# Second attention: mixing products in two parts, maxima in four places

## The reference, cut to what matters

```python
B, S, H = (2, 256, 512)             # the kernel gets x as 1 x 1024 x 512
hd = H // HEADS                      # 32 heads of 16
scale = 1.0 / np.sqrt(hd)
qkv = x @ attn_qkvw + attn_qkvb
...
scores = jnp.einsum('bhqd,bhkd->bhqk', q, k) * scale
probs = jax.nn.softmax(scores, axis=-1)
ctx = jnp.einsum('bhqk,bhkd->bhqd', probs, v)
```

## Time and profile before

| | us |
|---|---|
| runs of the kernel before | 1608.85, 1609.5, 1614.17 |
| their median | 1609.5 |
| span of the profiled execution, first to last instruction | 1606.4 |
| median less span | 3.1 |

### The profile page before, as it was taken

The page is one execution under the profiler, slowest core; times in us unless marked ns, Lnnn a source line. Parts: engine busy times, 40 slices in busy tenths (PEclk is TensorE's granted clock), DMA queues, the critical chain, the costliest instruction groups (busy, mean ns, idle before and its releaser), DMA issues. The chain is left out here.

```text
span 1606.4 us, 22430 instructions
## 1 busy us (share of the span) xinstructions
PE 1492.6 (93%) x8030; PEld 981.8 (61%) x8030; DVE 1023.0 (64%) x2013; ACT 821.6 (51%) x1487; POOL 291.7 (18%) x276
## 2 busy tenths in 40 slices
PE   6866999999999999977979999899899999999998
PEld 4645777766677776656868888787453333333355
DVE  5744666666666666643553343364687998999646
ACT  5325666666666666632221212223316777777854
POOL 2762111111211111100000000001410243342221
PEclk9987999999999999998989999999998999999999
DMA  4142222121212221124312111105730444430001
GB/s 138 53 193 73 76 75 69 64 69 64 69 63 80 90 70 40 34 86 156 105 63 75 59 60 40 53 1 152 189 67 5 68 81 79 80 67 15 19 11 53
DMA packets 63154, 116.57 MB, mean 73 GB/s; under 512 B 12814, under 2 KB 32398, under 8 KB 61758
## 3 DMA queue, kind: packets, MB, share of 16 engines
q1 hardware_dynamic: 62692, 114.23, 24.4%
q10 hardware_dynamic: 288, 0.79, 0.3%
q0 software_dynamic: 64, 0.11, 0.0%
HBM read 82.78 MB, written 29.66 MB: 70 GB/s over the span
## 5 line engine op out<-in xcount | busy, mean ns | idle before, releaser
L1882 DVE TENSOR_REDUCE ah_minus_half<-ah_ring 128x1 f32<-128x512 f32 x512 | 321.8, 680 | 58.5 <-PE ah_ring L1788 57.1
L968 DVE CUSTOM_DVE_ANT_0 mh_score<-mh_score,mh_mask 128x128 f32<-128x128 f32 (+7 forms) x256 | 195.9, 765 | 179.1 <-PE mh_score L781 179.0
L1852 ACT ACTIVATE ah_probs<-ah_score 128x1024 f32<-128x1024 f32 x256 | 248.7, 1024 | 69.5 <-PE ah_score L1805 68.8
L890 ACT ACTIVATE mh_probs<-mh_score,mh_minus_max 128x128 f32<-128x128 f32 (+7 forms) x256 | 189.8, 741 | 39.7 <-DVE mh_minus_max L968 35.7
L1788 PE MATMUL ah_ring<-ah_k_stack,ah_q_stack 48*128 48x512 f32 x512 | 179.1, 464 | 13.9 <-DMA ah_k_stack<-qk_scratch 5.5
L1788 PEld LDWEIGHTS ah_ring<-ah_k_stack,ah_q_stack 48*128 48x128 f32 x512 | 79.0, 187 | 173.1 <-DVE ah_minus_half L1882 158.9
L1041 POOL TENSOR_TENSOR h_lo<-mh_pe,h_hi 64x512 fp32r<-64x512 f32 x64 | 81.8, 1278 | 459.0 <-ACT h_hi L876 455.4
L1805 PE MATMUL ah_score<-ah_q_stack,ah_k_stack 49*128 49x512 f32 x512 | 156.5, 444 | 4.6 <-DMA ah_q_stack<-ah_rows 2.9
L779 PE MATMUL mh_score<-shared,h_hi 128*128 128x512 f32 (+3 forms) x384 | 152.0, 396 | 3.0 <-ACT mh_probs L890 2.9
L1820 PE MATMUL ah_mix<-ah_probs,ah_v 128*32 128x512 f32 x1024 | 139.0, 615 | 0.6 <-ACT ah_probs L1852 0.6
L781 PE MATMUL mh_score<-shared,h_lo 128*128 128x512 f32 (+3 forms) x384 | 133.0, 346 | 0.0
(11 more groups left out here) (227 smaller groups left out, 2898.7 us busy)
## 6 DMA issues: line engine op xcount, KB each, us to landing
mh_w<-in_w_pairs SPq DMA_DIRECT2D x16, 896.0 KB, 5.6
x<-in_w_inner SPq DMA_DIRECT2D x14, 768.0 KB, 4.2
pe_scratch<-fr_pe_out SPq DMA_DIRECT2D x4, 2048.0 KB, 6.6
mh_pe<-pe_scratch SPq DMA_DIRECT2D x16, 512.0 KB, 4.0
mh_spread<-inverse_scratch SPq DMA_DIRECT2D x64, 128.0 KB, 2.9
a_scratch<-mh_mixed SPq DMA_DIRECT2D x32, 256.0 KB, 2.4
x<-a_scratch SPq DMA_DIRECT2D x8, 1024.0 KB, 6.3
qk_scratch<-ai_ring SPq DMA_DIRECT2D x32, 256.0 KB, 2.8
```

Source lines behind the costliest of these rows:

```text
L890: nc.scalar.activation(probs[:, s % 2, 0:width], score_ps[s % 2][:, base:base + width], ACT.Exp, bias=minus_max[:, s % 4:s % 4 + 1], scale ...
L968: nc.vector.tensor_tensor_reduce(out=scores, in0=scores, in1=mask[:, S - width:S], scale=-1.0, scalar=3e38, op0=ALU.add, op1=ALU.min, accu ...
L1852: nc.scalar.activation(probs[:, 2 * (u % 2) + c, :], score_ps[c][:].rearrange("p e n -> p (e n)"), ACT.Exp, scale=MHA_SCALE).then_inc(prob ...
L1882: nc.vector.reduce_max(minus_half[:, m:m + 1], ring[:, m % 3, :], AX.X, negate=True).then_inc(max_taken, 1)
```

## The change

`mix` gets a part: part 0 does columns 0 to 255 of the queries, part 1 columns 256 to 511, each with all four heads. The rounds get a fourth stage: stages 2 and 3 are the two parts. The maxima of a round are divided over four places, one ahead of each stage after the first and one left over for the next round. The waits stand ahead of part 0 alone, the signal `mixed` behind part 1. The accumulation's start flag is set in part 0 of the first key tile only.

```diff
         def maxima_before(n, stage):
 
             now, then = maxima_at(n), maxima_at(n + 1)
-            return (now, min(now + (then - now + 1) // 2, then), min(now + (3 * (then - now) + 2) // 4, then))[stage]
+            return now - (-stage * (then - now) // 4)
...
-            def mix(g, u):
+            def mix(g, u, part):
                 a = g % DEPTH
                 half, j = divmod(u, NT)
-                if (g, u) == (0, 0):
+                if (g, u, part) == (0, 0, 0):
                     pe.wait_ge(ones_set, 1)
-                if j == 0:
+                if j == 0 and part == 0:
                     wait(pe, out_taken, NHALF * g + half)
-                wait(pe, probs_ready, 2 * (NUNIT * g + u + 1))
+                if part == 0:
+                    wait(pe, probs_ready, 2 * (NUNIT * g + u + 1))
+                first, end = part * BANK // 2, (part + 1) * BANK // 2
                 for head in range(4):
                     p, c = divmod(head, 2)
                     rows = slice(32 * head, 32 * head + 32)
-                    last = nc.tensor.matmul(mix_ps[rows, :], v[j][:, 4 * g * 2 * HD + 32 * head:4 * g * 2 * HD + 32 * head + 32], probs[:, 2 * (u % 2) + c, p * BANK:(p + 1) * BANK],
-                                            start=j == 0, stop=j == NT - 1)
-                last.then_inc(mixed, 1)
+                    values = slice((4 * g + head) * 2 * HD, (4 * g + head + 1) * 2 * HD)
+                    last = nc.tensor.matmul(mix_ps[rows, first:end], v[j][:, values],
+                                            probs[:, 2 * (u % 2) + c, p * BANK + first:p * BANK + end],
+                                            start=j == 0 and part == 0, stop=j == NT - 1, skip_group_check=True)
+                if part == 1:
+                    last.then_inc(mixed, 1)
...
             for n in range(UNITS + 1):
-                for stage in range(3):
+                for stage in range(4):
                     while done < maxima_before(n, stage):
                         one_maximum(done)
                         done += 1
                     if n < UNITS and stage < 2:
                         scores(n // NUNIT, n % NUNIT, stage, done % 2)
-                    if n and stage == 2:
-                        mix((n - 1) // NUNIT, (n - 1) % NUNIT)
+                    if n and stage >= 2:
+                        mix((n - 1) // NUNIT, (n - 1) % NUNIT, stage - 2)
```

## The result

| | us |
|---|---|
| profiled execution of the changed kernel | 1622.03, span 1620.2 (predicted: 1624, span 1621.1) |
| its first four runs | 1622.03, 1639.26, 1658.19, 1713.94; median 1648.7 |
| four runs beside it of the kernel before | 1608.85 to 1621.77, median 1611.8 |
| ratio | 1.0114, interval 1.0057 to 1.017 |
| four more runs of it (after_again) | 1670.08, 1671.72, 1689.38, 1759.74; median 1680.6 |

The explanation can't leave them out: the time of all eight runs follows their mean granted clock, from 0.964 (1622 us) through 0.937 (1658) to 0.874 (1760), while 70 runs of the kernel before, in the three sets of experiments, lie at 0.953 to 0.970 and none took over 1626 us. So there are two results.

What follows compares the result with a forecast made beforehand. TensorE was taken to bind short units and a round trip through VectorE long ones; 15.4 + 1.3 - 2 = +14.7 us took the span from 1606.4 to 1621.1, plus 3.1 to 1624 us, range 1608 to 1635.

Steps and rivals of the forecast that it cites:

- the step that carried the sum: Maxima in four places: TensorE binds every unit, 2.69 and 2.455 us against 2.70 and 2.12, together +15.4 us.
- Rival A: Second attention's mixing: ring product's weights load while the first part still streams; 1590 to 1602 us; chance 0.11.
- Rival C: Second attention: TensorE can't be fed 24 matmuls and 24 loads per long unit; over 1640 us; chance 0.06.
- regular units: Second attention's loop, 114 intervals: 66 long units at -0.7 us and 48 short ones at +16.1, together +15.4.
- first units at the half clock: First three units, at the lower clock: 1.9 us more, of which 1.3 was not yet in the sum.
- turns of the maxima: VectorE's transposes and join at a turn cost the new order about as much: 0.86 us against 0.42 slack.
- waits for rows: Four waits of scores for rows of maxima, 4.1 us, shrink by about 2 because units are longer.
- The 3.1 us from span to time: Whole kernel: median of the runs lies 3.1 us over the profiled span, so 1621.1 becomes 1624.
- rival B: Second attention: half the extras (6 us) vanish by VectorE slack, lone ring nears 0.33 (-10 us); 1606 to 1614; chance 0.13.
- The step on places where the stage isn't regular: Second attention's 16.7 us of extras: first units at the lower clock +1.3, turns unchanged, waits for rows -2.
- The chance over 1635: Times above the range: TensorE that can't be fed, over 1640 us, chance 0.06.
- One sign: Second attention's loop: idle time on VectorE before nearly every maximum, near 0.3 and 0.66 us.

Runs made afterwards that it cites:

- parts_adjacent: Changed kernel with the maxima in the places of before, so no ring product between the two mixing parts; 1608.68 us, ratio 0.9998 to the kernel before.
- two_between: Changed kernel with the maximum ahead of the first part moved between the parts, so two ring products stand there; 1673.75 us, ratio 1.0307 to the kernel before.
- The pair of runs without any fall: Kernel before and changed kernel, each with extra products in the first rounds and joined maxima sent ahead of the stack reloads; 1602.45 and 1611.3 us.
- before_rows_first: Kernel before with only SyncE's order changed: joined maxima sent ahead of the reloads of the stacks; 1603.67 us, ratio 0.9959.
- ring_of_two: Kernel before with two ring places instead of three from the loop's first unit on; 1702.92 us, ratio 1.0546.
- long_rounds_split: Changed kernel's two parts and four places only in rounds with four maxima, rounds with three as in the kernel before; 1613.74 us, ratio 1.0019.
- after_filled_start: Changed kernel with two extra, overwritten products ahead of each ring product and score stage of the first round and a half; 1616.39 us, ratio 1.005.
- score_between: Two parts only in rounds of four maxima, with a ring and a score product between them; other rounds as in the kernel before; 1606.09 us, ratio 0.9985.
- ring_in_scores: Kernel before, mixing whole; in rounds of four maxima the fourth ring product goes between the second stage's two score products; 1613.34 us, ratio 1.0022.

## Why the prediction was right, and where it wasn't

**What was right.** The direction, and the step that carried the sum. A part holds TensorE for 0.57, the lone ring product 0.42, slots 0.90 and 1.13, units 2.70 and 2.47 for the predicted 2.69 and 2.455; TensorE binds every unit and VectorE's idle time takes the place of the old one. Rival A, ring loads under the running part, falls with the loads at 1298.07 and 1299.06: each stands 0.57 behind the part's first load. Rival C, TensorE that can't be fed, falls with 85.0 of 85.0 us busy at the predicted pace. parts_adjacent and two_between put the price where the prediction had it: the division free, the extra change between the kinds of product 0.42 to 0.43, with one ring product or with two.

**The sum, term by term**, from the starts of the 115 mixings with maxima in both profiles (114 intervals; what a unit takes over its regular time is put to the event in it). In the new order 67 of them are long and 47 short, not 66 and 48 as the prediction has it for both orders, since the fourth maximum of a long round stood ahead of its mixing and now stands behind it; that is worth 0.2 us:

| term | predicted | measured |
|---|---|---|
| regular units | +15.4 | +16.6 (67 x 2.698 and 47 x 2.469, against 66 x 2.702 and 48 x 2.122) |
| first units at the half clock | +1.3 | -0.5 (4.35 over regular, was 4.84; the clock came back after 10.2 us, not 13.7) |
| turns of the maxima | 0 | -5.0 (2.9, was 7.9) |
| waits for rows | -2 | -3.0 (0.7, was 3.75; that at 1403.87 counts in the next line) |
| second fall of the clock, 1400.5 to 1420.9 | not in the sum | +7.4 |
| sum | +14.7 | +15.4 (15.5 by the rounded terms) |

So 1622.03 beside 1624 is in part luck. The turns of the maxima were mis-sized, a second fall of the clock was left out, and the two largely cancel. The 3.1 us from span to time were wrong too: they set the span of one execution beside the median of others, and in every run that has both the time lies 1.7 to 1.9 us over the span, here 1.8. The turns were put at "about as much" as before, from a slack of 0.42 us against 0.86 of work. The trace shows the slack handing the delay on over several units: VectorE falls behind at a turn and catches up, and TensorE waits less. This is the first half of rival B. The pair of runs without any fall shows what the edit then costs: 16.6 for the regular units, less 5.6 at the turns (7.7 us over regular with the old order, 2.1 with the new), is about the 11.1 us measured there. It is still slower, and B holds at a third of its full 16 us: its first half (6 us) nearly, its second (a lone ring product of 0.33) not at all, with 0.42.

**What was wrong.** The step on places where the stage isn't regular treated the half clock as a fixed piece of the trace of before: three units, 13 us. It is the term that decides most runs. The chance over 1635 was held for TensorE that can't be fed; yet seven of eight runs of the changed kernel lie above 1635, with a median of all eight near 1671. The range was built from costs of instructions, and the one thing taken over from the trace of before without a bound was how long the clock stays down. What a unit takes there was right (4.75 worked out, 4.74 measured); the stretch lasted 153.6 us in place of 13.7 in the profile of after_again. One sign failed as well: idle time of VectorE stands before 104 of the 410 maxima, not before nearly every one. The forecast holds for a run in which the clock comes back as it did before, and this was the exception.

**What is shown of the clock and what isn't.** Shown: behind the first units and up to the end of the maxima, the profiles of all orders have eleven falls. Ten of them follow, within 2.0 us, a wait of 1.27 to 3.00 us of a score product for rows of maxima, the eleventh (before_rows_first) a wait for VectorE; with the waits for rows taken away and the start filled no run of twelve took over 1615.3 us. Such a wait doesn't always bring a fall (1.47 and 1.57 us above), so it is no rule. Not shown: what brings the clock back. PE is busy for 153.89 of 154 us at half and for 305.69 of 306 at full, ring_of_two is less busy and comes back after 47.8 us, and the ends of the long stretches (1361, 1346, 1494, 1542) have no event in common that the traces show. The stretches of 137 us and more stand only in orders with nothing but ring products between the two parts (the changed kernel, two_between, long_rounds_split, after_filled_start); score_between, with a ring and a score product there, has none, but with ten runs of each that isn't clear of chance.

## What to carry to other kernels

Where two kinds of matmul that divide the array differently alternate, count the changes between them before their sizes: halving a product was free, while the one product put between the halves took 0.42 us (a slot among its own kind takes 0.235) and made the short units 0.35 us longer. An idle engine that a page shows may be the result of the bound, not the bound; read the engine that it waits for in one place, load by load. And look for the short waits of TensorE ahead of each fall of its granted clock: here one DMA, moved ahead of reloads for a later group, was worth 6.6 us (0.41%, interval 0.24 to 0.59%).

## What the runs showed of the hardware

The granted clock can stay at its lower level (1.2 GHz) for 137 to 178 us while the profile shows TensorE busy nearly all the time, in an order that in another profile, without the waits, runs at the upper level (2.4 GHz) for all of 306 us. The Trainium skill, page TensorE: Matmul & The Clock Gate, Part 1, says that the gate goes by how busy TensorE has been; by the busy time of the profile (153.89 of 154 us at half, in after_again) this trace doesn't show it. One us at half cost 0.37 us here, less than one half.

A ring product that starts behind a part of the mixing, or behind a wait for its place, takes 0.42 to 0.43 us up to the next mixing load whether it is alone (1298.07), paired with another (two_between, 1297.65) or with a score (score_between, 1296.81; ring_in_scores, 1292.68): behind such a start, the second product of a pair is free.
